# Down projection of the last two pairs in seven products for all eight pieces, and the first tiles loaded from two queues

## The reference

```python
x = L0_attn_x                                  # (8, 512, 512), float32
xn = layernorm(x)
# linear attention without decay, 16 heads of 32
q, k, v = xn @ Wq.T + bq, xn @ Wk.T + bk, xn @ Wv.T + bv
context = (elu(q) + 1) * cumsum((elu(k) + 1) * v, axis=tokens) * SCALE
s = context @ Wo.T + bo
# gated feed forward, 512 -> 2048 -> 512, with Walsh-Hadamard transforms around it
u = fwht(xn * SU_ug) / 64
hidden = silu(u @ W_gate.T * (Wscale_gate * 64)) * (u @ W_up.T * (Wscale_up * 64))
d = fwht(hidden * SU_dp) / 64 @ W_down.T * (Wscale_dp * 64)
out = x + s * silu(d)
```

## Time and profile before

| what | value |
|---|---|
| median of 3 runs | 1291.22 us (1289.54 to 1293.17) |
| profiled execution, whole | 1291.18 us |
| profiled execution, span from first to last instruction | 1289.4 us |
| TensorE busy | 1259.5 us, 98% |
| VectorE busy | 936.1 us, 73% |
| ScalarE busy | 618.3 us, 48% |
| GpSimd busy | 108.9 us, 8% |
| granted TensorE clock, mean | 1.000 |
| HBM read, written | 171.64 MB, 53.50 MB |

### The profile page before, as it was taken

One profiled execution on the slowest core, in us unless ns is written; L12 is line 12 of the kernel. 1 busy time (PEld: TensorE's weight loads), 2 busy tenths in 40 slices (PEclk: granted clock), 3 DMA queues, 4 the chain that ended last, 5 costly groups with the idle time before them and its releaser, 6 DMA issues.

```text
span 1289.4 us, 16166 instructions
## 1 busy us (share of the span) xinstructions
PE 1259.5 (98%) x5896; PEld 570.7 (44%) x5896; DVE 936.1 (73%) x1417; ACT 618.3 (48%) x912; POOL 108.9 (8%) x159
## 2 busy tenths in 40 slices
PE   5999999999999999999999999999999999999998
PEld 3544444444444444444444444444444444444443
DVE  6989989878656777777883778776773767775724
ACT  5894655532245655552334555554233655454212
POOL 1000001131210000120022001000001000000001
PEclk9999999999999999999999999999999999999999
DMA  9534775777757356575378333323526433332423
GB/s 370 224 131 125 242 215 186 241 251 292 229 205 237 113 196 231 220 251 196 131 229 257 134 128 134 131 99 103 205 93 196 145 117 116 113 129 76 130 95 103
DMA packets 65472, 226.21 MB, mean 175 GB/s; under 512 B 7408, under 2 KB 17904, under 8 KB 50800
## 3 DMA queue, kind: packets, MB, share of 16 engines
q1 hardware_dynamic: 41840, 170.64, 36.7%
q0 software_dynamic: 16272, 42.48, 11.9%
q10 hardware_dynamic: 7280, 12.06, 2.7%
HBM read 171.64 MB, written 53.50 MB: 175 GB/s over the span
## 4 chain that ended last, share of the span: by engine, by line
PE 78%; DVE 9%; issue 5%; ACT 5%; DMA 3%; SPq 0%; DVEq 0%; ACTq 0%
PE bank L2450 40%; PE bank L2636 13%; PE bank L2330 12%; PE bank L2516 7%; PE bank L2541 2%; PE bank L2661 2%; ACT work L1229 1%; ACT work L1232 1%; DMA h_all<-scr_f 1%; DVE work L1675 1%; PE bank L2375 1%; PE bank L2561 1%; DVE work L1659 1%; DVE work L1665 1%; DVE work L1702 1%
## 5 line engine op out<-in xcount | busy, mean ns | idle before, releaser
L2450 PE MATMUL bank<-xops,ring 128*128 128x512 f16 x2772 | 603.2, 379 | 7.4 <-DVE work L1702 2.6
L2450 PEld LDWEIGHTS bank<-xops,ring 128*128 128x128 f16 x2772 | 269.4, 98 | 340.2 <-issue 11.1
L2330 PE MATMUL bank<-xops,ring 128*128 128x512 f16 x1008 | 225.2, 379 | 0.5 <-DVE ring L1831 0.5
L1212 ACT ACTIVATE work<-bank 128x512 f32<-128x512 f32 x198 | 117.8, 595 | 214.7 <-PE bank L2450 200.2
L1659 DVE TENSOR_TENSOR work<-bank,work 128x512 f32<-128x512 f32 x198 | 133.4, 686 | 113.0 <-PE bank L2450 99.8
L2636 PE MATMUL bank<-h_all,ring 128*128 128x512 f16 x768 | 166.8, 379 | 0.2 <-DVE work L1659 0.2
L2330 PEld LDWEIGHTS bank<-xops,ring 128*128 128x128 f16 x1008 | 98.1, 98 | 123.6 <-issue 9.1
L2636 PEld LDWEIGHTS bank<-h_all,ring 128*128 128x128 f16 x768 | 75.0, 98 | 91.0 <-DVE work L1659 0.7
L1259 ACT ACTIVATE h_all<-work 128x512 f16<-128x512 f32 x116 | 70.6, 624 | 62.6 <-DVE work L1702 62.5
L1711 DVE TENSOR_TENSOR h_all<-work,h_all 128x512 f16<-128x512 f32 x116 | 79.3, 686 | 5.7 <-ACT h_all L1259 4.4
L1665 DVE SCALAR_TENSOR_TENSOR work<-work 128x512 f32<-128x512 f32 x64 | 44.1, 690 | 51.2 <-ACT work L1232 50.8
(11 more groups left out here) (284 smaller groups left out, 1323.4 us busy)
## 6 DMA issues: line engine op xcount, KB each, us to landing
ring<-scr_g SPq DMA_DIRECT2D x72, 1024.0 KB, 4.8
ring<-scr_d SPq DMA_DIRECT2D x15, 1024.0 KB, 5.8
scr_g<-ring SPq DMA_DIRECT2D x22, 512.0 KB, 4.4
h_all<-in_ug_t SPq DMA_DIRECT2D x8, 1024.0 KB, 12.9
ring<-in_down_t SPq DMA_DIRECT2D x6, 1024.0 KB, 6.5
scr_g<-ring POOLq DMA_DIRECT2D x12, 512.0 KB, 5.7
work<-in_x_t SPq DMA_DIRECT2D x6, 1024.0 KB, 7.0
scr_g<-h_all POOLq DMA_DIRECT2D x12, 512.0 KB, 2.9
```

Of the source, the lines that this page charges most:

```text
L1212: act.activation(tile(g, j), chain_bank(g)[:, :], ACT.Copy).then_inc(copied, 1)
L2330: mm = pe.matmul(plain_bank(g, j)[:, :], at[:, s, 2 * dh + kk, r, :], xops[:, kk, xs, PLAIN_B[dh][c], :], start=(n == 0), stop=(n == len(t ...
L2450: mm = pe.matmul(to[:, :], weight_of(slot, s, b, kk), at, start=(a == 0 and m in (P1, P2, P5)), stop=(a == 5), skip_group_check=True)
```

## The change

The seven products take all eight pieces (`SEVEN` = `FP` = 8), and `rest` with its four products, its ring slot (R11) and its sum "22a" is no longer called. Products have 24 matmuls. Their order becomes P1, P2, P6, P7, P4, P5, P3, each for d = 0 and 1. Pieces 6 and 7 need homes for three summed tiles each; these are places of the token operands `xops` (T2 or T3, and B21) that group 21 has read for the last time. `hidden_sums_high` therefore waits, for piece 6, for product P2 of group 21, and for piece 7 for P7; it is two instructions instead of one, and so is `hidden_sums_low`. Piece 7's sums stand in `last_sums`. Product (d, P1) waits for `h_ready` of piece 7's C11 tile, P2 for that of its C21 tile, P6 for piece 7's sums, and P3 for the sum "22" of its own d.

`seven_and_o` is ordered anew on VectorE: sums "11", the first half of the next pair's operands, sum "22" of d = 0, the adds of the second half, sum "22" of d = 1, the rest of the second half, sums "12". On ScalarE the next pair's `x_high` and `t_high` stand between the SiLUs, whose order is C11, C21, C22, C12. `x_high` of pair 3 also waits for P4 of the down stage, `load_x(3)` for piece 7's sums, and `load_last_res` for P5. The units behind pair 1 are eight instead of six.

At the head, tiles 1, 3, 5 and 7 of the eight first tiles are loaded from ScalarE's queue, tiles 0, 2, 4 and 6 from SyncE's, and the identity matrix stands behind the weight of K.

```diff
-GATE_ORDER = [(d, j) for j in (C11, C22, C21, C12) for d in range(2)]
+GATE_ORDER = [(d, j) for j in (C11, C21, C22, C12) for d in range(2)]
...
-SEVEN_FROM, SEVEN = 2, 6
-REST = FP - SEVEN
...
-DOWN_SLOTS = (P1, P2, P6, P7, P5, R11, P4, P3)
-DOWN_ORDER = [(d, m) for ms in ((P1, P2), (P6,), (P7,), (P5,), (R11,), (R21,), (R22,), (R12,), (P4,), (P3,))
-              for d in range(2) for m in ms]
+SEVEN_FROM, SEVEN = 2, FP
+DOWN_SLOTS = (P1, P2, P6, P7, P4, P5, P3)
+DOWN_ORDER = [(d, m) for m in DOWN_SLOTS for d in range(2)]
...
+        def homes_late(i, s):
+            b = (T2, T3)[i - IN_RES]
+            return xops[:, :, s, b, :], xops[:, i - IN_RES, s, B21, :]
...
             def load_x(p):
                 sp.wait_ge(h_ready, 32 * p)
+                if p > SEVEN_FROM:
+                    sp.wait_ge(hidden_sums_ready, sums_of_hidden(p - 1, SEVEN - 1))
...
-            for c in FIRST_CHUNKS:
-                for t in range(TB):
-                    sp.dma_start(x_ln[:, TB * c + t, :], x[c, t * P:(t + 1) * P, :]) \
-                        .then_inc(x_first_loaded[TB * c + t], 16)
-                if c == FIRST_CHUNKS[0]:
-                    sp.dma_start(ident[:, :], ident_in).then_inc(ident_loaded, 16)
+            for t in range(0, 2 * TB, 2):
+                c, at = FIRST_CHUNKS[t // TB], t % TB
+                sp.dma_start(x_ln[:, TB * c + at, :], x[c, at * P:(at + 1) * P, :]).then_inc(x_first_loaded[TB * c + at], 16)
...
+                at = 4 * (g % 3)
+                if i < IN_RES:
+                    act.activation(home(i)[:, :, HI, :], work[:, at:at + 3, :], ACT.Copy).then_inc(hidden_sums_hi, 1)
+                    return
+                act.wait_ge(product_done, products_to(p, GROUPS - 1, (P2, P7)[i - IN_RES]))
+                two, third = homes_late(i, HI)
+                act.activation(two, work[:, at:at + 2, :], ACT.Copy)
+                act.activation(third, work[:, at + 2, :], ACT.Copy).then_inc(hidden_sums_hi, 1)
...
                 ctx_high(p, 1)
-                if p < PAIRS - 1:
-                    x_high(p + 1, 0)
-                    t_high(p + 1, 0)
-                    x_high(p + 1, 1)
-                    t_high(p + 1, 1)
                 for d, j in GATE_ORDER:
+                    if p < PAIRS - 1:
+                        if (d, j) == (0, C21):
+                            x_high(p + 1, 0)
+                        elif (d, j) == (0, C22):
+                            t_high(p + 1, 0)
+                            x_high(p + 1, 1)
+                        elif (d, j) == (0, C12):
+                            t_high(p + 1, 1)
                     seven_gate(p, d, j)
...
+            for t in range(1, 2 * TB, 2):
+                c, at = FIRST_CHUNKS[t // TB], t % TB
+                act.dma_start(x_ln[:, TB * c + at, :], x[c, at * P:(at + 1) * P, :]).then_inc(x_first_loaded[TB * c + at], 16)
             square_attn(K)
...
             def seven_and_o(p):
+                for d in range(2):
+                    seven_add(p, d, "11")
                 if p < PAIRS - 1:
                     x_sums(p + 1, 0)
                     t_low(p + 1, 0)
+                seven_add(p, 0, "22")
+                if p < PAIRS - 1:
+                    x_adds(p + 1, 1)
+                seven_add(p, 1, "22")
+                if p < PAIRS - 1:
+                    x_low(p + 1, 1)
+                    t_low(p + 1, 1)
                 for d in range(2):
-                    seven_add(p, d, "22a")
...
+                    seven_add(p, d, "12")
...
                 if m == P1:
-                    pe.wait_ge(h_ready, 32 * p + 4 * SEVEN)
+                    pe.wait_ge(h_ready, 32 * p + 4 * SEVEN - 3)
                     wait_taken(pe, p, GROUPS - 2 + d, C21)
                 elif m == P2:
+                    pe.wait_ge(h_ready, 32 * p + 4 * SEVEN - 1)
                     pe.wait_ge(summed, 3 * nth(p, GROUPS - 2 + d) + 1)
                 elif m == P5:
                     pe.wait_ge(summed, 3 * nth(p, GROUPS - 2 + d) + 3)
+                elif m == P4:
+                    pe.wait_ge(seven_copied, down_copied_to(p, d, P7))
+                elif m == P3:
+                    pe.wait_ge(seven_summed, down_summed_to(p, d, "22"))
```

More of the change, by code:

```diff
@@ L220, in slot_of @@
         return RING[n % len(RING)]
-    return LATER_RING[(LOADS * (p - SEVEN_FROM) + n) % len(LATER_RING)]
+    return LATER_RING[(loads_of(p) * (p - SEVEN_FROM) + n) % len(LATER_RING)]
 def dmas_of(p, n):
-    return 2 if p >= SEVEN_FROM and GROUPS <= n < GROUPS + 2 * KB else 1
-ALL_LOADS = [(p, n) for p in range(1, PAIRS) for n in range(LOADS)]
+    return 2 if p >= SEVEN_FROM and GROUPS <= n < GROUPS + len(DOWN_SLOTS) else 1
+ALL_LOADS = [(p, n) for p in range(1, PAIRS) for n in range(loads_of(p))]
 def loads_into(p, n):
@@ L733, in load_seven @@
                         sp.wait_ge(unit_stored[u], 16 * UNITS)
[L734 to L739, removed]
                 to = ring[:, slot, 0:512 * SEVEN].rearrange("p (d n) -> p d n", d=2)
@@ L747, in load_seven @@
                 sp.dma_start(to[:, :, 0:1024], scr_d[2 * half, :, 2 * r:2 * r + 2, :]).then_inc(slot_loaded[slot], 16)
-                sp.dma_start(to[:, :, 1024:256 * SEVEN], scr_d[2 * half + 1, :, 2 * r:2 * r + 2, 0:1024 - 256 * REST]) \
+                sp.dma_start(to[:, :, 1024:256 * SEVEN], scr_d[2 * half + 1, :, 2 * r:2 * r + 2, :]) \
                     .then_inc(slot_loaded[slot], 16)
@@ L764, in load @@
                         sp.wait_ge(piece_stored[s], 16 * len(range(s, GROUPS, 3)))
[L765 removed]
+                if p >= SEVEN_FROM and GROUPS <= n < GROUPS + len(DOWN_SLOTS):
                     load_seven(p, n)
@@ L768, in load @@
                 if p >= SEVEN_FROM:
-                    piece = n if n < GROUPS else n - 2 * KB
+                    piece = n if n < GROUPS else n - len(DOWN_SLOTS)
                 else:
@@ L866, in _ @@
             for p in range(1, PAIRS):
-                for n in range(LOADS):
+                for n in range(loads_of(p)):
                     load(p, n)
@@ L1267, in hidden_sums_high @@
                     act.wait_ge(phi_made, 16 * p + 16)
-                elif i >= 4 and p < PAIRS - 1:
+                elif 4 <= i < IN_RES and p < PAIRS - 1:
                     act.wait_ge(stats_taken, 2 * p + 2)
-                three = work[:, 4 * (g % 3):4 * (g % 3) + 3, :]
-                act.activation(home(i)[:, :, HI, :], three, ACT.Copy).then_inc(hidden_sums_hi, 1)
+                at = 4 * (g % 3)
+                if i < IN_RES:
+                    act.activation(home(i)[:, :, HI, :], work[:, at:at + 3, :], ACT.Copy).then_inc(hidden_sums_hi, 1)
[4 more added lines that the diff above has]
+                act.activation(third, work[:, at + 2, :], ACT.Copy).then_inc(hidden_sums_hi, 1)
             def take(p, g, j):
@@ L1729, in hidden_sums_low @@
                 dve.tensor_tensor(at[:, LO, :], tile(g, C12), at[:, HI, :], ALU.subtract).then_inc(h_ready, 1)
-                three = work[:, 4 * (g % 3):4 * (g % 3) + 3, :]
+                a = 4 * (g % 3)
                 dve.wait_ge(hidden_sums_hi, sums_of_hidden(p, i))
-                dve.tensor_tensor(home(i)[:, :, LO, :], three, home(i)[:, :, HI, :], ALU.subtract) \
-                    .then_inc(hidden_sums_ready, 1)
+                if i < IN_RES:
+                    dve.tensor_tensor(home(i)[:, :, LO, :], work[:, a:a + 3, :], home(i)[:, :, HI, :], ALU.subtract) \
+                        .then_inc(hidden_sums_ready, 1)
+                    return
+                (two_high, third_high), (two, third) = homes_late(i, HI), homes_late(i, LO)
+                dve.tensor_tensor(two, work[:, a:a + 2, :], two_high, ALU.subtract)
+                dve.tensor_tensor(third, work[:, a + 2, :], third_high, ALU.subtract).then_inc(hidden_sums_ready, 1)
             def use(p, g, j):
@@ L2224, in last_sums @@
                 hidden_low(p, g, C21)
+                if p >= SEVEN_FROM:
+                    for part in range(2):
+                        hidden_sums(p, FP - 1, part)
+                    hidden_sums_low(p, FP - 1)
                 hidden_low(p, g, C12)
@@ L2480, in group @@
                     for d, m in DOWN_ORDER[1:]:
[L2481 to L2484, removed]
+                        seven(p, d, m)
                 elif g + 1 == GROUPS:
@@ L2518, in seven @@
                                        stop=(i == SEVEN - 1 and n == 2), skip_group_check=True)
[L2519 to L2542, removed]
                 mm.then_inc(seven_done, 1)
```

50 lines of the change are left out of this document (28 added, 22 removed).

## The result

The changed kernel is slower: 1302.68 us median of 4 runs (1301.56 to 1303.54), against 1291.16 us (1289.54 to 1293.17). The ratio is 1.0088, with a 95% interval from 1.0071 to 1.0105. The forecast was 1297.8 with a range up to 1302.0: right in direction, 4.9 us short in size, and 0.7 us above the range.

What follows compares the result with a forecast made beforehand. TensorE was taken as the bound nearly everywhere. Pair 2 +5.5, pair 3 +1.3, units +0.5 and head -0.7 gave +6.6 us, so 1291.2 became 1297.8, range 1292.3 to 1302.

Steps and rivals of the forecast that it cites:

- Matmuls saved: Down stage of pairs 2 and 3: 336 matmuls instead of 348 a pair, 2.59 us each, 5.2 us in all.
- Stall A: First down product of pairs 2 and 3: TensorE waits 3.9 us (bounds 2.9 and 4.5) for piece 7's C11 tile.
- Between, pair 2: Pair 2, after the first down product: piece 7's sums hidden with 6 us to spare, context work paced by TensorE.
- Stall B: At (0, P3), pair 2 only: TensorE waits 4.5 us (bounds 3 and 7) for sum "22" of d = 0.
- The units: Behind pair 1: two more units' loads and stores cost +0.5 us, between 0 and 1.5.
- The head: First tiles, loads split over two queues: -0.7 us (between -1.5 and +0.5), first transpose near 13.8.
- Rival 3: Pairs 2 and 3, worse: Stall B near 7 (+2.5), ring's loads (+1), Stall A at upper bound (+1.2): about 1302; chance 0.12.
- the ring's loads: Term of Rival 3: the ring's loads behind the units' stores cost 1.5 us (+1).

Runs made afterwards that it cites:

- the pair of kernels: The changed kernel without either stall, with the new head, 1285.07 us, against the same with all first-tile loads on SyncE's queue as before, 1285.41 us.
- The filled stall: The changed kernel with both stalls, but TensorE does 16 matmuls into an unread bank during the first, in pairs 2 and 3: 1298.44 us.

## Why the prediction was wrong

- **Matmuls saved: right.** 5872 against 5896, and the kernel with neither stall is 6.3 us faster than the one before: 5.2 for the matmuls, 0.8 for the two small waits; 0.3 is left open.
- **Stall A: place, releaser and order right.** 3.63 us against 3.9, in both pairs. The lower bound of 2.9 was met to 0.02 us by the kernel that adds the wait alone. Piece 6's sums added 0.75, where some 0.9 had been taken.
- **Between, pair 2: right.** Piece 7's sums ended at 914.3 and were hidden. The second half of the context was paced by the copy of P7 (941.71), as forecast.
- **Stall B: right.** 3.85 us against 4.5, in pair 2 alone, behind the same sum; moving that sum removed it.
- **The units: no cost, where +0.5 had been taken. The head: no gain, where -0.7 had been taken.** Together -0.2 was forecast; the trace has +0.1 in the head and -0.46 for the ring wait that is gone. The first transpose came at 14.72 us, where 13.8 had been forecast. The estimate of the head went by VectorE's bound and took too little off for K's weight on the same DMA engines. The sentence of the Trainium skill ("DMA: Bandwidth & Descriptors", section "Issuing engines are not separate DMA queues") that issuing on several engines saves only the time of issuing was borne out here: all tiles were issued 2.3 us earlier, and the pair of kernels is 1285.07 against 1285.41 us. ScalarE's tiles did leave at once, as the prediction had it: its table load, at 0.73 us before, moved behind the four issues to 2.62.
- **The step that failed is the price of the stalls in the sum.** "Stall A is 3.9 us" and "Stall B is 4.5 us" were entered as idle time alone, as though TensorE went on behind them at its old pace. The missing term is the granted clock: 2.8 + 1.5 + 2.9 = 7.2 us in the profiled execution. The idles themselves were 1.2 us shorter than forecast (11.1 against 12.3), which hid a part of the gap. Without the term the same sum, with the measured sizes, is +5.2 instead of +12.4. The filled stall shows that the term is one of its own (4.2 us measured for A in both pairs, 4.3 by the trace), and the kernels without stall A that it goes with the idle.
- **Rival 3 is near the measured time by luck.** Its terms add up to 1302.5 (the text rounds it to 1302, and the range ends there), 0.2 us from the measured 1302.68, but none of them came: stall B was 3.85 us and not 7, A 3.63 and not 4.5, and the ring's loads cost nothing.

The Trainium skill has the rule that I left out: "TensorE: Matmul & The Clock Gate", section "What's actually happening", says of the clock that "the default state is throttled, and activity releases the throttle". The windows above (0.50 at the end of the first stall and behind it) and the filled stall (5.35 us instead of 8.16 for the same matmuls) agree with it. The kernel before had a row for the price as well, at its start. TensorE comes to its first transposes after 14.58 us without work, and 24 of them, one every 0.22 us, take twice as long as the eight at 21.53, one every 0.11:

```profile
14.58 5.24 PE L2550 MATMUL bank<-ident,work 128*128 128x128 f32 x24 [14.58 <-DVE work L1576]
...
21.53 1.04 PE L2550 MATMUL bank<-ident,work 128*128 128x128 f32 x8
```

The views give a clock of 1.00 for both, but that is no reading for the first: the trace's record of the clock begins at 19.58 us. In the kernel without stalls it begins at 18.04, and there the same 24 transposes go over from 0.21 to 0.11 us at that moment. So TensorE had worked at half pace behind a long idle in the kernel before too, and half pace on the matmuls behind each stall could have been a term of the sum, or at least a rival.

What stays open: what decides whether the clock falls in a given execution. With the same idle of 3.63 us it fell at both places in one kernel's profile and at neither in another's; with 2.88 us it fell at both, a moment after the idle. How long it stayed at half differed too, 1.5 to 2.9 us of loss behind idles of nearly the same length.

## What to carry to other kernels

- In this kernel, whose TensorE hardly rests, a new stall of some 3 us mostly had two prices, the idle and the slower matmuls behind it. Here the second was 1.5 to 2.9 us each, up to about three quarters of the first. Work saved in matmuls (5.2 us) is easily given back.
- When a product takes in a late operand, place the wait at the first matmul that reads it, not at the head of the product: 21 matmuls in front of it hid 3.63 us at no cost. Together with the moved sum this made the change worth having (1285.07 us).
- On an engine with a fixed order, place an add whose product is done ahead of a long preparation. Where a stall can't be removed, matmuls into an unused bank kept the clock here (1298.44 against 1302.68 us).

## What the runs showed of the hardware that was not expected

- Behind an idle of TensorE of 3.63 us the granted clock was 0.52 for 6.0 us of work (15 matmuls instead of 28), behind 3.85 us 0.50 for 5.8 us.
- An idle of 2.88 us was enough twice in one profile; two idles of 3.63 us were not in another. Two idles of 1.65 us left the clock alone in the profile.
- The half clock can begin after the idle: behind 2.88 us it came 1.1 us after TensorE had started again. At the start of the kernel TensorE's first transposes were 0.22 us apart and later ones 0.11.
